# Decoder layer on one core: self-attention batch by batch, softmax normalised on the head outputs, residual in seven 128-token tiles

## The reference

```python
# 1 self-attention, 16 heads of 32, key j hidden where j - i > 32
q, k, v = x @ wq.T, x @ wk.T, x @ wv.T
out = softmax(mask(q @ k.T * 32**-0.5)) @ v @ wo.T
# 2 cross attention to the context, 16 heads of 128, q and k RMS-normalised
out = softmax(rms(x @ Wq) @ rms(ctx @ Wk).T * 128**-0.5) @ (ctx @ Wv) @ Wo
# 3 a shared gated MLP (704) plus the best 2 of 8 experts (352), weighed by a router
out = shared(x) + sum(w_e * expert_e(x))
```

## Time and profile before

| | |
|---|---|
| runs | 1204.36 us median of 3 (1202.34 to 1205.1) |
| profiled execution, its own time | 1207.62 us |
| its span, first to last instruction | 1205.9 us |
| PE busy | 1102.7 us (91%), mean granted clock 0.949 |
| DVE, ACT, POOL busy | 672.2, 464.5, 442.6 us |

### The profile page before, as it was taken

How to read it: one execution, slowest core, us unless ns; L and a number is a source line. 1 busy time by engine, 2 the same in 40 slices (tenths; PEclk the granted TensorE clock), 3 DMA queues, 4 the chain that set the end, 5 groups by cost and what they waited for, 6 DMA issues and landing times. The chain is left out here.

```text
span 1205.9 us, 19600 instructions
## 1 busy us (share of the span) xinstructions
PE 1102.7 (91%) x7034; PEld 931.3 (77%) x7034; DVE 672.2 (56%) x1186; ACT 464.5 (39%) x934; POOL 442.6 (37%) x410
## 2 busy tenths in 40 slices
PE   6988856999999999999999999999849799999994
PEld 5666535899999999999999999998738665566583
DVE  3678852567766766666667667666652211111246
ACT  4444411555554454455454544554321011111200
POOL 0456630665533533535335335333123500000172
PEclk9999955999999999999999999999969899999997
DMA  7120020232322323223213232222173579999432
GB/s 252 36 78 2 2 77 27 87 138 96 126 95 89 105 85 100 95 83 104 91 71 111 92 99 104 77 76 78 52 240 132 235 278 332 349 344 331 187 97 96
DMA packets 45751, 155.27 MB, mean 129 GB/s; under 512 B 3881, under 2 KB 3881, under 8 KB 42641
## 3 DMA queue, kind: packets, MB, share of 16 engines
q1 hardware_dynamic: 43456, 147.21, 35.1%
q0 software_dynamic: 2240, 7.34, 1.8%
HBM read 130.04 MB, written 22.66 MB: 127 GB/s over the span
## 5 line engine op out<-in xcount | busy, mean ns | idle before, releaser
L803 DVE TENSOR_TENSOR xa_kT_lo<-xa_turn_ps,xa_kT_hi 128x750 fp32r<-128x750 f32 x64 | 60.2, 940 | 121.1 <-ACT xa_kT_hi L731 121.1
L694 POOL TENSOR_TENSOR xa_probs<-xa_probs,xa_inv_sum 112x750 f32<-112x750 f32 x64 | 98.7, 1543 | 69.6 <-DVE xa_inv_sum L852 69.6
L86 PE MATMUL xa_k_ps<-xa_wk_hi,ctx_hi 128*125 128x256 f32 x384 | 112.0, 292 | 10.5 <-DVE xa_wk_lo L562 9.8
L679 POOL TENSOR_TENSOR xa_k_ms<-xa_k_ss,xa_sum_eps 125x6 f32<-125x6 f32 x64 | 12.8, 200 | 265.2 <-DVE xa_k_ss L818 265.0
L87 PE MATMUL xa_k_ps<-xa_wk_hi,ctx_lo 128*125 128x256 f32 x384 | 109.8, 286 | 0.0
L88 PE MATMUL xa_k_ps<-xa_wk_lo,ctx_hi 128*125 128x256 f32 x384 | 109.8, 286 | 0.0
L1559 PE MATMUL ex_gu_ps<-ex_raw,ex_xb 128*128 128x352 f32 x336 | 103.0, 459 | 0.7 <-ACT ex_xb L1284 0.7
L924 PE MATMUL xa_c_ps<-xa_probsT_hi,xa_nat 125*128 125x224 f32 x384 | 93.1, 276 | 3.6 <-ACT xa_probsT_hi L747 3.6
L925 PE MATMUL xa_c_ps<-xa_probsT_hi,xa_nat 125*128 125x224 f32 x384 | 92.9, 275 | 0.0
L682 POOL TENSOR_TENSOR xa_k_inv<-xa_k_ms,neg_half 125x6 f32<-125x6 f32 x64 | 85.0, 1328 | 8.4 <-POOL xa_k_ms L679 6.7
L753 ACT ACTIVATE xa_probs<-xa_scores_ps,xa_bias,xa_q_scale 112x375 f32<-112x375 f32 x128 | 83.9, 660 | 10.2 <-DVE xa_bias L828 7.0
(11 more groups left out here) (261 smaller groups left out, 3066.5 us busy)
## 6 DMA issues: line engine op xcount, KB each, us to landing
xa_nat<-ctx_split SPq DMA_DIRECT2D x56, 750.0 KB
ex_raw<-in_w_units SPq DMA_DIRECT2D x23, 1408.0 KB, 7.6
ex_raw<-in_w_units SPq DMA_DIRECT2D x23, 768.0 KB, 6.7
ctx_split<-xa_nat SPq DMA_DIRECT2D x8, 750.0 KB
sorted_x<-ex_y_sb SPq DMA_DIRECT2D x1, 5376.0 KB, 17.7
ex_x_nat<-sorted_x SPq DMA_DIRECT2D x21, 256.0 KB, 6.1
sorted_y<-ex_y_sb SPq DMA_DIRECT2D x21, 256.0 KB, 6.3
xa_wq_raw<-in_w_pairs SPq DMA_DIRECT2D x8, 512.0 KB, 10.4
```

Source lines behind the costliest of these rows:

```text
L86: pe.matmul(out, st_hi, mv_hi, start=first, stop=False)
L694: pool.tensor_tensor(probs[0:T, u % 2], probs[0:T, u % 2], inv_sum[0:T, u % 2, :].unsqueeze(2).broadcast_to([T, 2, KV]), ALU.mult).then_in ...
L803: dve.tensor_tensor(kT_lo[:, :, 0:KV], turn_ps[:, :, 0:KV], kT_hi[:, :, 0:KV].bitcast(F32), ALU.subtract).then_inc(sem["kT_lo_done"], 1)
```

## The change

In self-attention batches become the outer loop and quads the inner one. All four quads' queries and keys are kept (`qT`, `kT` with QUADS), and the twelve projections of quads 1 to 3 are made whole in slots 0 to 3 (`PROJ`, `PROJ_SLOTS`). The values of batch b are made in two halves in slots 4b-1 and 4b, always in `proj_ps`. Probabilities are no longer multiplied by reciprocals: TensorE spreads each head's reciprocals over its 32 rows with a matmul against the identity (L566 of the changed kernel), ACT copies them, and DVE multiplies the head outputs by them (`o_norm`); both halves then come from that array, the low one on POOL. Outputs of neighbouring batches lie side by side in `oT_hi` and `oT_lo` (batch 4 twice), so that the output projection takes 128 tokens and gathers the four quads in PSUM: 28 groups of three products and seven adds, instead of 32 and 32. Each tile's norm and turn follow in the loop, in slots 4t+6 to 4t+13 (`ends_tile`). Context splits move to slots 8 to 14 and 30 to 36 and the output weights' to slots 3 to 6; some arrays share memory. In cross attention norm and turn at the start are gone, and seven tiles a pair are projected and added instead of eight (`tile_of`: none for the second batch). In the experts' block `resid` itself has the seven tiles, the 14 copies are gone, and gathers go to an array `got` of their own.

```diff
 def turn_stages(nc, env, sem, norm_done, banks):
-        for c in range(DC):
-            mm = pe.transpose(banks[b % 2][:, c * T:(c + 1) * T], resid[0:T, b, c * P:(c + 1) * P], ident[0:T, 0:T])
+        for c in range(DC):
+            mm = pe.transpose(banks[t % n][:, c * P:(c + 1) * P], resid[:, t, c * P:(c + 1) * P], ident[:])
@@ self_attention, constants
+        PROJ = [(0, 0, 0), (0, 0, 1), (0, 1, 0), (0, 1, 1), (1, 0, 0), (1, 0, 1), (1, 1, 0), (2, 0, 0), (2, 0, 1), (1, 1, 1),
+                (2, 1, 0), (2, 1, 1), (3, 0, 0), (3, 0, 1), (3, 1, 0), (3, 1, 1)]
+        PROJ_SLOTS = {0: (4, 7), 1: (7, 10), 2: (10, 15), 3: (15, 16)}
+        ctx_slots = {8: 0, 10: 1, 12: 2, 14: 3, 30: 4, 32: 5, 34: 6, 36: 7}
+        wo_slots = {3: 0, 4: 1, 5: 2, 6: 3}
+        def ends_tile(u):
+            b, q = divmod(u, QUADS)
+            return b - 1 if q == QUADS - 1 and 1 <= b < B else None
@@ gpsimd
-                    pool.tensor_tensor(probs[0:T, u % 4], probs[0:T, u % 4],
-                                       inv_sum[0:T, u % 2, :].unsqueeze(2).broadcast_to([T, QUAD, T]),
-                                       ALU.mult).then_inc(sem["probs_done"], 1)
+                    wait(pool, "oT_hi_done", u + 1)
+                    pool.tensor_tensor(places(oT_lo, q, b), o_copies(u), places(oT_hi, q, b).bitcast(F32),
+                                       ALU.subtract).then_inc(sem["oT_lo_done"], 1)
@@ scalar, in slot s, u = s - 2 then u = s - 1
+                    wait(act, "inv_spread", u + 1)
+                    act.copy(inv_rows[:, u % 2, :], o_ps[:, P:P + T]).then_inc(sem["inv_copied"], 1)
+                b, part = divmod(s - 1, QUADS)
+                if part == 0 and 1 <= b < B:
+                    copy_values(b)
+                t = ends_tile(s - 6)
+                if t is not None:
+                    wait(act, "v_ready", min(t + 2, B))
+                    turn_high(act, t)
@@ vector, behind mask and maximum of u = s
+                    wait(dve, "o_ready", u + 1)
+                    dve.tensor_tensor(o_norm[:, u % 2, :], o_ps[:, 0:T], inv_rows[:, u % 2, :],
+                                      ALU.mult).then_inc(sem["o_norm_done"], 1)
+                t = ends_tile(s - 6)
+                if t is not None:
+                    turn_low(dve, t)
@@ tensor
+                    for r in range(QUAD):
+                        mm = pe.matmul(o_ps[r * SA_DH:(r + 1) * SA_DH, P:P + T],
+                                       inv_sum[0:T, u % 2, r:r + 1].broadcast_to([T, SA_DH]), ident[0:T, 0:T],
+                                       start=True, stop=True)
+                    mm.then_inc(sem["inv_spread"], 1)
+                b, part = divmod(s + 1, QUADS)
+                if 1 <= b < B and part < 2:
+                    values(b, (2 * part, 2 * part + 1))
+                t = ends_tile(s - 6)
+                if t is not None:
+                    wait(pe, "v_copied", min(t + 4, B))
+                    turn(pe, t)
@@ cross_attention
-            ln_apply(dve)
-                    for b in range(B):
-                        turn(pe, b)
-                    pe.wait_ge(sem["turn_lo"], B)
+        def tile_of(u):
+            b = u % B
+            return None if b == 1 else max(b - 1, 0)
+                    t = tile_of(u)
+                    if t is not None:
+                        part = slice(t * P, (t + 1) * P)
+                            mm = three_products(pe, y_ps[:], oT_hi[:, h, part], oT_lo[:, h, part], wo_hi[:, h, :],
@@ experts
-            for a, z in pieces:
-                sp.wait_ge(env["cross_norm"]["ln_done"], a // T + 1)
-                sp.dma_start(rows[a % P:a % P + z - a, a // P, :],
-                             resid[a % T:a % T + z - a, a // T, :]).then_inc(sem["rows_moved"], 16)
```

More of the change, by code:

```diff
@@ L201, in wait, with proj_done, all_proj, proj_bank @@
                 eng.wait_ge(sem[name], n)
[L203 to L221, removed]
+        def proj_done(q, g):
+            return max(PROJ.index((q, g, 0)), PROJ.index((q, g, 1))) + 1
+        def all_proj(q):
+            return max(n for n, (quad, _, _) in enumerate(PROJ) if quad == q) + 1
+        def proj_bank(n):
+            return (proj_ps, y_ps)[n % 2]
+        def copies_in(s):
+            first, last = PROJ_SLOTS.get(s - 1, (0, 0))
+            late = [last - 1] if last > first else []
+            first, last = PROJ_SLOTS.get(s, (0, 0))
+            return late, list(range(first, last - 1))
+        def wv_part(buf, c):
+            at = HALF * KV + c % 2 * D
+            return buf[:, c // 2, at:at + D]
+        def wo_part(buf, q):
+            return buf[:, q // 2, q % 2, :]
+        def places(buf, q, b):
+            view = buf[:, q, :].rearrange("p (r t) -> p r t", t=T)
+            if b == HALF:
+                return view[:, 0:SPAN:HALF, :]
+            at = b % HALF
+            return view[:, at:at + 1, :]
+        def o_copies(u):
+            n = 2 if u // QUADS == HALF else 1
+            return o_norm[:, u % 2, :].unsqueeze(1).broadcast_to([P, n, T])
+        def tile_cols(t):
+            at = t * P - (HALF * T if t >= HALF else 0)
+            return slice(at, at + P)
+        def ends_tile(u):
+            b, q = divmod(u, QUADS)
+            return b - 1 if q == QUADS - 1 and 1 <= b < B else None
         def ctx_cols(k):
@@ L309, in _ @@
+                act.copy(V[0:T, b % 3, :], proj_ps[0:T, :]).then_inc(sem["v_copied"], 1)
+            split_hi("wq", 0)
+            split_hi("wk", 0)
             for c in range(DC):
                 wait(act, f"xT_{c}_loaded", 16)
-                act.copy(xT_hi[:, c, :], xT_raw[:, c, :]).then_inc(sem["xT_hi_done"], 1)
+                for g in range(2):
+                    cols = slice(g * HT, (g + 1) * HT)
+                    act.copy(xT_hi[:, c, cols], xT_raw[:, c, cols]).then_inc(sem["xT_hi_done"], 1)
@@ L869, in slot @@
                 if s == 0:
-                    for b in range(B):
-                        turn_low(dve, b)
                     split_lo(dve, 0, 0, "wq", wq_raw, wq_hi, wq_lo)
@@ L1286, in _ @@
             up_high(0, 0)
-            for b in range(B):
-                turn_high(act, b)
+            for t in range(TILES):
+                turn_high(act, t)
             down_high(0, 0)
@@ L1474, in _ @@
         def _(pe):
-            for b in range(B):
-                turn(pe, b)
-            pe.wait_ge(sem["turn_lo"], B)
+            for t in range(TILES):
+                turn(pe, t)
+            pe.wait_ge(sem["turn_lo"], TILES)
             def logits_T():
```

450 lines of the change are left out of this document (243 added, 207 removed).

## The result

| | before | changed |
|---|---|---|
| median, same chip | 1204.55 us (7 runs) | 1212.34 us (7 runs, 1207.75 to 1218.1) |
| ratio, 95% interval | | 1.0064 [1.0043, 1.0084] |
| profiled execution, its span | 1207.62 us, 1205.9 us | 1211.68 us, 1209.9 us |
| PE busy, mean granted clock | 1102.7 us, 0.949 | 1100.3 us, 0.959 |

The change makes the kernel 0.64% slower; I had forecast 1202 us, 0.2% faster. The range of 1190 to 1214 us held the time, the forecast case did not happen. The mean clock rose although the kernel became slower, so it does not show the trouble; the stages do.

What follows compares the result with a forecast made beforehand. TensorE was taken to bound cross attention and the self-attention loop, VectorE its late slots. Self-attention 14.8 us longer, first queries 10.9 and cross attention 6.5 shorter: -2.6 us, median 1202 us, range 1190 to 1214.

Steps and rivals of the forecast that it cites:

- the forecast case: Whole kernel: the summed terms hold, median 1202 us, its own range 1197 to 1207; chance 0.5.
- loop start: Ahead of the self-attention loop: one batch of values less, 2.8 us saved, start at 24.7 us.
- slots 4 to 12: Self-attention loop: values slots 3.6 us by TensorE, others 2.8 by VectorE, context splits partly covered; sum 30.4 us.
- slots 13 to 29: Self-attention loop: batches of four slots at 15.3 us each, with slot 29 and two context splits 67.7 us.
- drain: End of self-attention: slots 30 and 31 take 6.7 us, the chain behind them to the next block 12.8.
- The turn chain: Every fourth loop slot: TensorE's turn waits for the values copy, delaying VectorE's next mask; 5.05 us mask to mask.
- the rival to which I had given 0.2: Self-attention loop: the turn chain hides, 11.5 us less, giving 1190 us; chance 0.2.
- half clock inside the loop: Slots 25 to 31: TensorE's gaps halve its clock for one and a half batches, 13 us more, 1215; chance 0.15.
- the sign of being wrong that I had named: Self-attention loop: the prediction is wrong if TensorE's granted clock (PEclk) falls before slot 28.
- The transition: Next block's start to first queries: eight applies and eight turns gone, queries 10.9 us sooner, clock left at 0.54.
- Cross attention: One output projection of eight less per pair of heads gains 0.77 us each, 6.5 us taken in all.
- my 1.3 for the third slot of a batch: Self-attention loop, third slot of each batch: GpSimd's shift priced at 1.3 us, from its average of 1.29.

Runs made afterwards that it cites:

- e7: Changed kernel with the values copy first among ScalarE's operations of its slot instead of fifth; 1206.79 us, ratio 0.9997 to the kernel before.
- e3: Changed kernel with each tile's turn, high half and low half one slot later; 1202.25 us, ratio 0.9962 to the kernel before.
- e2: Changed kernel with 91 unused TensorE products in slots 5 to 7, 10, 11, the turn slots and two behind them; 1208.93 us, ratio 1.0013 to before.
- e1: Changed kernel with 17 unused TensorE products in the waits of slots 5 to 7; 1206.39 us, ratio 0.9999 to the kernel before.
- e8: Changed kernel with the last context split in slot 35 instead of 36; 1210.55 us, ratio 1.0041 to the kernel before.
- e5: Changed kernel with six unused products per pair of heads put back in cross attention; 1217.46 us, ratio 1.0080 to the kernel before.
- c1: The changed kernel run again without any edit; 1212.77 us, ratio 1.0072 to the kernel before.

## Why the prediction was right or wrong

Step by step, in the profiled executions (us):

| step | forecast | measured | off |
|---|---|---|---|
| loop start | 24.7 | 24.1 | -0.6 |
| slots 0 to 3 | 40.1 | 39.25 | -0.9 |
| slots 4 to 12 | 30.4 | 34.0 | +3.6 |
| slots 13 to 29 | 67.7 | 70.3 | +2.6 |
| drain | 19.5 | 21.6 | +2.1 |
| block to first queries | 25.1 - 10.9 = 14.2 | 15.1 | +0.9 |
| queries to experts | 688.8 - 6.5 = 682.3 | 680.7 | -1.6 |
| experts | 324.4 | 324.8 | +0.4 |

Rounded, these add to the 6.6 us between the forecast's span, 1205.9 - 2.6 = 1203.3, and 1209.9. The loop start and the row from queries to experts vary from execution to execution at the same code (21.3 to 24.1 and 680.7 to 685.9 us), so their differences say little.

- **The turn chain was right** in place, order and size (5.05 against 5.10). e7 and e3 take 6.7 and 9.6 us of it out of the loop. It was in the forecast, so it explains nothing of the miss; but without it the change would have been a gain, as e3's 0.9962 shows. Even there the time is 1202 us, not the 1190 of the rival to which I had given 0.2.
- **The step that failed is the clock.** The sum left the loop at full rate, a term put at nothing; my rival "half clock inside the loop", with 0.15, is what happened, and so did the sign of being wrong that I had named, PEclk falling before slot 28. My reason against it, that the slots before 135 us are as full as these, did not hold by my own figures: hardly a gap in the slot of the earlier trace rows, 12.1 us of matmuls in a batch of 15.3. The rival gave 1215 for a fall in the last batches; the falls came early, in slots 7 and 15 to 16, and the last batches kept 1.00. I had priced it by the turn slots, and looked for poor slots by those alone; the poorest were 5 and 6, whose emptiness stood in my own list of what they hold. The two stretches cost 4.8 us, 2.1 in slot 7 and 2.7 in slots 14 to 16. Without them, by this estimate, the kernel would be within some 3 us of the kernel before (7.8 - 4.8); e2, which has neither, is at 1.0013. That TensorE's poor slots bring the first fall is shown by e1; what decides on the second stays open. The time lies inside the range all the same, but the range's upper part stood for a cold end of the loop, so that is luck.
- **Slots 4 to 12, warm, were 1.5 us too low** (31.9 in e1 against 30.4): VectorE's splits of the output weights wait for ScalarE ahead of the mask. I had counted their place, not their wait; slot 7 alone takes 5.2 us warm instead of 3.6.
- **The drain was 2.1 too low.** By the changed kernel's trace the last output projection starts 12.7 us into it where the forecast has 6.7 + 4.4 = 11.1. From there to the last add it takes 1.4 instead of 2.7, since the clock was still full, although a context split stands ahead of the add. From the add to the end of the last low half it takes 6.4 instead of 4.7: the power 1.5 instead of 0.9, and the 0.9 of overlap that I had taken off did not come. The 0.8 that e8 saves is the split behind the chain, which the forecast had (0.9).
- **The transition was right** but for the first loads, whose key weight's high half began 4.1 us into the block instead of 3.1.
- **Cross attention: mechanism right** (e5), 0.6 to 0.7 us a pair instead of the 0.77 behind my 6.5. Of the 8.1 us measured, 2.3 stand ahead of the first scores (19.0 us behind the first query instead of 21.3), where TensorE was at half rate throughout before and only in part after; that is the clock, not the change. In c1 this stage took 682.7 us, 6.2 less than before.
- GpSimd's shift in the loop fell from a mean of 1.289 us to 0.996:

```profile
L328 POOL TENSOR_TENSOR sa_masked<-sa_masked,sa_row_max 112x448 f32<-112x448 f32 x30 | 29.9, 996 | 30.7 <-DVE sa_row_max L457 30.7
```

Single shifts show where the 0.3 us come from. Before, 18 of 32 took 0.94 us at most, most of them beside the residual add, which reads PSUM; the other 14 took 1.31 to 2.16 us, and beside each ran the low half of a weight's or context's split (L355, L409), which reads two arrays in SBUF. In the changed kernel 26 took 0.94 at most, one took 1.63 beside such a split, and five 1.11 to 1.18 beside an apply of the norm (L489). Where the shift started first, the low half was the longer one: 0.96 us at 74.14 against 0.69 at 70.78, above. This agrees with the rule on shared memory interfaces that the prediction took from the Trainium skill ("GPSIMD Engine Reference", Specifications). But it is not the new reads from PSUM that spare the shift: fewer splits run beside it. In the late slots of before it took 0.93 us already, so my 1.3 for the third slot of a batch was too much, and the batches came out at 15.6 us all the same.

## What to carry to other kernels

When work moves out of a pipelined loop's slots, list for each slot what TensorE still has in it, and look at the poorest ones next to each other before counting a loop at full clock. An operation for which nobody hurries (a turned tile's low half) must not stand ahead of one in the critical chain on an in-order engine while its input is not ready: one slot later cost 1.2 us in the drain and gave back 9.6 in the loop, besides a cold stretch. And place the copy that frees a shared PSUM bank first on its engine, not last.

## What the runs showed of the hardware

The granted clock fell to the level of 1.2 GHz at 72 us although no wait of TensorE ahead of it was longer than 0.8 us; it was busy 2.73 us of the 4 before. Ahead of the second fall the longest wait was 1.1 us. The Trainium skill ("TensorE: Matmul & The Clock Gate", HAM oscillation) tells of falls behind long waits for data; here short waits in a row sufficed, while the turn slots from 17 on, each of which would begin cold by the prediction's reading of it, kept 1.00 (113 to 165 us). And whether a poor stretch brings a fall is not set by the kernel alone: slots 13 to 15 are the same in c1 and e8, with one cold stretch in the first and none in the second, whose loop began 0.9 us earlier. What decides it was not tested; it may be part of why single executions of the changed kernel lie between 1207.75 and 1218.1 us, at mean clocks of 0.963 and 0.952.
